# The 48 pixels of each row of f start at column 1 instead of column 2 of rows of 52, in an input-dependent 3x3 convolution on Trainium2

## The reference

```python
xn = group_norm(x)                                   # 32 groups
f = relu(einsum('oc,nchw->nohw', Wc, xn) + bc)       # 64 channels, 48x48
gk1 = relu(mean(xn, (2, 3)) @ Wc.T + bc)
g_kern = (gk1[:, :, None] * Wkk + bkk)               # 3x3 per channel
sk = relu(einsum('oc,nckl->nokl', Wc, block_max_3x3(xn)) + bc)
dynW = relu(einsum('oj,ncjkl->nockl', Wck, stack(g_kern, sk)) + bck)
y = conv3x3(f, dynW, padding=1) + b_ad               # each image has its own weights
out = x + einsum('oc,nchw->nohw', Wf, y) + bf
```

## Time and profile before

| | |
|---|---|
| median of 3 runs | 516.32 us (513.82 to 516.66) |
| profiled execution, its own time | 513.47 us |
| its span, first to last instruction | 511.7 us |
| TensorE busy (matmul) | 489.6 us, 96% |
| ScalarE, VectorE, GpSimd busy | 427.9, 418.8, 296.0 us |
| HBM traffic over the span | 296 GB/s |

### The profile page before, as it was taken

How to read it: one execution, slowest core, us unless ns; L and a number is a source line. 1 busy time by engine, 2 the same in 40 slices (tenths; PEclk the granted TensorE clock), 3 DMA queues, 4 the chain that set the end, 5 groups by cost and what they waited for, 6 DMA issues and landing times.

```text
span 511.7 us, 19208 instructions
## 1 busy us (share of the span) xinstructions
PE 489.6 (96%) x8338; PEld 383.4 (75%) x8338; DVE 418.8 (82%) x653; ACT 427.9 (84%) x486; POOL 296.0 (58%) x231
## 2 busy tenths in 40 slices
PE   4898999999999999999999999999999999999993
PEld 2353765578888888878888868888888888888881
DVE  6878778988888898888888978888898888888544
ACT  4778899989999999999999989999999999985231
POOL 5223775455677555557765545677555557765543
PEclk9798999999999999999999999999999999999998
DMA  8935678999999999999999998999899999964467
GB/s 340 420 120 199 202 278 308 366 340 329 331 352 298 344 343 358 315 341 315 317 335 338 356 359 305 328 330 315 323 363 366 323 313 327 320 264 157 153 266 295
DMA packets 48868, 158.01 MB, mean 309 GB/s; under 512 B 4752, under 2 KB 15888, under 8 KB 48784
## 3 DMA queue, kind: packets, MB, share of 16 engines
q1 hardware_dynamic: 48784, 156.78, 85.4%
HBM read 75.94 MB, written 75.50 MB: 296 GB/s over the span
## 4 chain that ended last, share of the span: by engine, by line
PE 80%; ACT 2%; DVE 0%; DVEq 0%; issue 0%; ACTq 0%
PE ps L1120 31%; PE ps L1252 22%; PE ps L1220 21%; PE ps L1171 7%; ACT unused L610 1%; DVE X L850 0%; ACT unused L597 0%; ACT f_hi L689 0%; DVEq L153 0%; ACT f L695 0%; ACT Y L587 0%; ACT dyn_hi L708 0%; ACT dyn_b L710 0%; PE ps L1364 0%; ACTq L130 0%
## 5 line engine op out<-in xcount | busy, mean ns | idle before, releaser
L850 DVE SCALAR_TENSOR_TENSOR X<-ps,out_bias,X 128x960 f32<-128x960 f32 (+1 forms) x189 | 185.3, 1009 | 17.9 <-PE ps L1252 17.5
L1252 PE MATMUL ps<-Y,const 64*64 64x480 f32 (+1 forms) x1536 | 167.2, 487 | 0.0
L513 POOL TENSOR_TENSOR dyn_a<-const,pool_g 128x576 f32<-128x576 f32 x30 | 34.9, 1164 | 168.7 <-DVE pool_g L874 168.7
L597 ACT ACTIVATE unused<-X,neg_mean 128x2304 bf16<-128x2304 f32 x60 | 132.0, 2201 | 0.4 <-DVE neg_mean L989 0.4
L610 ACT ACTIVATE unused<-X 128x2304 bf16<-128x2304 f32 x60 | 126.8, 2114 | 0.0
L1220 PE MATMUL ps<-X,wcn_t 64*64 64x384 f32 (+1 forms) x1296 | 115.8, 486 | 0.3 <-issue 0.3
L926 DVE TENSOR_REDUCE feats<-X 128x6 f32<-128x1536 f32 x64 | 111.6, 1745 | 0.0
L1220 PEld LDWEIGHTS ps<-X,wcn_t 64*64 64x64 f32 x1296 | 86.0, 133 | 25.0 <-issue 3.9
L1252 PEld LDWEIGHTS ps<-Y,const 64*64 64x64 f32 x1536 | 80.4, 133 | 7.6 <-issue 2.1
L528 POOL TENSOR_TENSOR f_lo<-f,f_hi 128x1152 f16<-128x1152 f32 x32 | 71.2, 2226 | 20.4 <-ACT f L695 20.4
L1120 PE MATMUL ps<-f_hi,dyn_hi 64*64 64x480 f16 x1152 | 72.0, 374 | 3.8 <-ACT dyn_hi L716 2.4
(11 more groups left out here) (101 smaller groups left out, 538.3 us busy)
## 6 DMA issues: line engine op xcount, KB each, us to landing
X<-x SPq DMA_DIRECT2D x63, 1152.0 KB, 9.5
out<-X SPq DMA_DIRECT2D x61, 1152.0 KB, 8.8
out<-X SPq DMA_DIRECT2D x6, 480.0 KB, 3.5
stack<-f_hi SPq DMA_DIRECT2D x64, 32.5 KB, 2.5
stack<-f_lo SPq DMA_DIRECT2D x64, 32.5 KB, 5.6
X<-x SPq DMA_DIRECT2D x2, 576.0 KB, 7.0
upper<-f_hi SPq DMA_DIRECT2D x32, 32.5 KB, 4.0
out<-X SPq DMA_DIRECT2D x3, 192.0 KB, 2.9
```

The costliest lines, as they stand in the source:

```text
L597: nc.scalar.activation(unused[:, t], pixels(u, t), ACT.Square, scale=1.0 / SIDE, bias=neg_mean[:, n % 2, 1:2], accum_out=feats[:, (n + 1) ...
L850: nc.vector.scalar_tensor_tensor(out=out, in0=unit_psum(piece, bank, col), scalar=out_bias[:, t:t + 1], in1=out, op0=ALU.add, op1=ALU.add) ...
L1252: mm = nc.tensor.matmul(ps[rows, bank + q, col:col + width], wft[lanes, t, rows], Y[lanes, n % 2, at:at + width], start=True, stop=True)
```

## The change

Two constants. The rows stay 52 elements long, and the pixels move one column to the left; the padding that was 2 columns on each side is now 1 on the left and 3 on the right.

```diff
@@ -43,8 +43,8 @@
 REST_ROWS = HROWS - 2 * MAIN_ROWS
 REST = REST_ROWS * SIDE
 STACK_ROWS = 2 * (REST_ROWS + 1)
-LEFT = 2
-PITCH = LEFT + SIDE + 2
+LEFT = 1
+PITCH = LEFT + SIDE + 3
 RING = 7
 AHEAD = 4
```

## The result

| | before | after |
|---|---|---|
| median of 9 runs | 514.53 us (513.70 to 517.55) | 511.99 us (511.25 to 512.90) |
| profiled execution: time, span | 513.47, 511.7 us | 512.45, 510.6 us |

The ratio of the runs is 0.9942, 95% interval 0.9926 to 0.9958. The time lies in the stated range, and the direction was the one forecast; the forecast ratio, 0.9953, lies inside the interval. The forecast of the time itself, 513.9 us, is 1.9 us too high: it set out from a median of three runs, 516.32 us, and that of nine is 514.53. I had given "no measurable change" the larger chance (0.56) and "faster by over 0.5%" 0.38; the ratio came out on the other side of that line, 0.9950, which lies inside the interval too.

A forecast was written before the change was run, and what follows sets the result against it. TensorE was taken as the bound in 28 images; 72 ns from `conv_main` and 14 from `conv_rest`, 86 ns an image, gave 2.4 us, so the median 516.32 became 513.9 us (ratio 0.9953), range 510.6 to 516.7.

The forecast's parts named there:

- TensorE is the bound in 28 images: Chain of waits from 90.91 to 489.27 us: TensorE sets the pace, so its saving per image counts 28 times.
- The 8 ns of an off-grid window: `conv_main` matmuls: a 10-row window starting off the 4-byte grid takes 8 ns longer (bounds 7 and 8.4).
- the word count: TensorE window reads: 48 16-bit elements take 24 4-byte words on the grid, 25 off it, at 0.84 ns a word.
- The sum of 86 ns: Per image on tile (1,1): `conv_main` 72 ns plus `conv_rest` 14 ns saved (bounds 75 and 92), 14.71 to 14.62 us.
- the 72 ns of `conv_main`: `conv_main`, three terms an image, each from 6 off-grid taps to 3: 9 x 8 = 72 ns saved.
- The rule of the Trainium skill: Matmul steps: 202.5 ns per 480 columns wherever a window starts, a term 1.82 us, so this change gains nothing.
- Writers at an odd column cost nothing: ScalarE's `f_high` and GpSimd's `f_low` writing float16 from an odd column: 0 taken for each; `f_low` bounds 0 and a doubling.
- GpSimd's slack of 1.1 us: GpSimd's scaled Wc ends at 268.90 us, awaited by `project_f` at 270.04; a slower `f_low` is free under 1.1 us.
- Rival 1: ScalarE's handover of Y to `conv_main(0)` takes part of the gain: 54 ns an image, median 514.8 us; chance 0.17.
- Rival 2: `conv_main` short steps are short as middle taps, not by start column: time stays at 516.3 us; chance 0.06.
- Rival 3: GpSimd's `f_low` slowed by odd rows: if doubled, 1.1 us on every image, 545 us; chance 0.05.
- Rival 4: TensorE's first four images pass their gain on too: 2.9 us, 513.4 us; chance 0.12.

The follow-up runs named there:

- all five kernels: Before, changed, changed with 53-element rows, and dx = 1 windows moved to put all windows on or all off the 4-byte grid: images 14.518 to 14.797 us.
- all-on-grid kernel: Changed kernel with the dx = 1 windows also beginning at column 0 (wrong pixels for middle taps): median 511.93 us, ratio 0.9944 to the kernel before.
- quarter-store kernels: Stores except the last images' cut to a quarter of their pixels: kernel before 512.72 us, changed 509.67, changed with every window on the 4-byte grid 507.55.

## Why the prediction was right

- **TensorE is the bound in 28 images:** right. 28 x 95 ns = 2.66 us against 2.54 us between the medians. That the two agree so well is in part luck, since the stops cost the changed kernel more.
- **The 8 ns of an off-grid window:** right, shown by the kernels with none, half and all rows off the grid. It was a row's address that counted, as the word count had it. That TensorE fetches 4-byte words is the reading that gave the size; the runs show the cost of a row, 0.86 ns, and not the fetch.
- **The sum of 86 ns:** the mechanism was right and one term was too small, the 72 ns of `conv_main`, which measured 80 (95 less the 15 of `conv_rest`), and so over the bound of 9 x 8.4 = 76 ns. The rate fits all five kernels only as a mean of 0.86 ns a row; why single steps of the ladder go from 0.74 to 1.06 is open. An image of 95 instead of 86 ns accounts for 0.25 us of the difference between 0.9953 and 0.9942, which is 0.6 us; the rest is within the interval.
- **The rule of the Trainium skill** ("TensorE: Matmul & The Clock Gate", "Back-to-back issue gap"), columns / 2.4 + 2.5 ns: the trace agrees for windows on the grid, where 9 steps give 1.82 us and the all-on-grid kernel has 1.82. It is short by some 8 ns for each window off it: three of them make the 1.85 us of the changed kernel.
- **Writers at an odd column cost nothing:** right, 1.0005 alone. How far GpSimd's slack of 1.1 us really reaches was not tried.
- **Rival 1, the handover:** the wait came as described, in nearly every image, and cost nothing, as the argument against it said. It takes some 0.17 us of further delay to bite.
- **Rival 2, the tap's place:** refuted. **Rival 3, a slower GpSimd:** did not occur. **Rival 4:** 2.9 us is not excluded for the image work, since the quarter-store kernels differ by 3.05 us, but the first four images were not measured by themselves. The first steady `project_f` starts at 93.78 us before and 93.58 after, and with quarter stores at 93.73 and 94.90, so the start moves by more than the 0.4 us in question.
- **What I had not in the sum:** the stops in `project_f`. By the medians they cost the changed kernel some 0.5 us more than the one before, and in the kernel before they make over half of the runs' spread, which I had taken as given.

## What to carry to other kernels

A 3-wide window on 16-bit rows always has one column of one parity and two of the other: lay out the padding so that the two fall on 4-byte addresses, with an even pitch. Sort the durations of equal matmuls before costing a layout change; two groups 8 ns apart were visible in the trace before anything was changed. And where the DMAs are near full, a quicker engine may give its gain back as stops, as the all-on-grid kernel did: compare one unstopped image with the whole run, and cut the traffic to see which of them tells the truth.

## What was unexpected of the hardware

A 16-bit moving operand costs TensorE 0.86 ns more for each row that starts off the 4-byte grid, at the granted clock of 1.00; that is close to the 0.84 ns of one 4-byte element. Four tiles of the array ran so independently that one of them could start some 0.12 us late (0.03 in the changed kernel and 0.09 of added delay) in nearly every image at no cost. And with DMAs busy for 0.90 of the time TensorE stopped for up to 1.8 us at a time in a stage that waited for nothing that the profile shows, 1.1 to 5.5 us in a profile; at a share of 0.63 0.1 to 0.4 us was left.
